# Normalised rows, the mixer's update of X and the copies of last states moved from GpSimd to ScalarE

## The reference

```python
x = x + attn(_layernorm(x), Wq, Wk, Wv, Wo)     # 16 heads; keys: a window of 32 rows, and every 64th row
x = x + ffn(_layernorm(x), k0, k1, k2, s0, s1, s2)
x = x + mamba(_layernorm(x), ...)               # returns its own input plus the output: x appears twice
x = x + ffn(_layernorm(x), k0, k1, k2, s0, s1, s2)

def ffn(x): h = concat([x, -x]); 256 -> 512 -> 512 -> 128, weights of +1 and -1, relu(h) * 2 between
def mamba(x):                                    # E = 256 channels, N = 16 states
    xn = layernorm(x) * ln_g + ln_b
    u, z = split(xn @ W_in);  u2 = silu(causal_conv4(u) + conv_b)
    dt_lo, B, C = split(u2 @ W_xp);  dt = softplus(dt_lo @ W_dt + b_dt)
    h_t = exp(dt_t * A) * h_(t-1) + (dt_t * u2_t) * B_t        # for each of 256 x 16 states, t = 0..1023
    y_t = sum over states of h_t * C_t
    return x + res_scale * (((y + u2 * D) * silu(z)) @ W_out)
```

## Time and profile before

| | |
|---|---|
| median of 3 runs | 812.72 us (811.11 to 813.23) |
| the profiled execution | 811.52 us, of which the trace spans 809.7 |
| busy over the span | PE 89%, DVE 86%, POOL 82%, ACT 73% |
| granted TensorE clock, mean | 0.989 |
| DMA | 154.94 MB, 191 GB/s, 71.4% of 16 engines' span on the main queue |
| first scan starts, last scan ends | 129.8 us, 784.0 us |

### The profile page before, as it was taken

The page is one execution under the profiler, slowest core; times in us unless marked ns, Lnnn a source line. Parts: engine busy times, 40 slices in busy tenths (PEclk is TensorE's granted clock), DMA queues, the critical chain, the costliest instruction groups (busy, mean ns, idle before and its releaser), DMA issues. The chain is left out here.

```text
span 809.7 us, 22189 instructions
## 1 busy us (share of the span) xinstructions
PE 721.4 (89%) x7840; PEld 430.6 (53%) x7840; DVE 695.3 (86%) x1187; ACT 594.8 (73%) x1161; POOL 664.2 (82%) x824
## 2 busy tenths in 40 slices
PE   5999988998789999998999999899896889897887
PEld 3765655644455447545555456355452356453566
DVE  6977229999999989999889999999998989799983
ACT  5776698797788989887689978868667744764533
POOL 5143437998899989989999799899998999999961
PEclk9999999999999999999999999999999999998999
DMA  5000019888799668877777889889797899898950
GB/s 200 3 3 2 2 54 269 226 231 229 206 225 237 159 173 238 230 177 200 198 213 197 225 233 243 232 230 244 207 253 199 252 259 240 215 266 235 264 158 27
DMA packets 84177, 154.94 MB, mean 191 GB/s; under 512 B 9433, under 2 KB 10082, under 8 KB 84066
## 3 DMA queue, kind: packets, MB, share of 16 engines
q1 hardware_dynamic: 84066, 153.51, 71.4%
HBM read 142.46 MB, written 11.01 MB: 190 GB/s over the span
## 5 line engine op out<-in xcount | busy, mean ns | idle before, releaser
L1779 POOL TENSOR_TENSOR d<-d,cr 128x1024 f32<-128x1024 f32 x128 | 300.0, 2354 | 13.8 <-DVE d L1279 4.1
L1578 ACT ACTIVATE ps<-dt,An 128x512 f32<-128x512 f32 x256 | 173.7, 690 | 71.9 <-DVE d L1279 60.5
L1279 DVE TENSOR_TENSOR_SCAN d<-ps,hl,d 128x512 f32<-128x512 f32 x128 | 157.0, 1262 | 3.7 <-ACT ps L1578 3.3
L1279 DVE TENSOR_TENSOR_SCAN d<-ps,d 128x512 f32<-128x512 f32 x128 | 149.6, 1202 | 7.2 <-ACT ps L1578 6.5
L1267 DVE TENSOR_TENSOR d<-ps,d 128x512 f32<-128x512 f32 x184 | 118.5, 671 | 7.1 <-DMA d<-dud 7.1
L891 PE MATMUL ps<-h,w 128*128 128x512 f16 (+1 forms) x512 | 114.3, 373 | 3.5 <-DVE h L1224 2.8
L1766 POOL TENSOR_TENSOR d<-d,br 128x512 f32<-128x512 f32 x72 | 91.5, 1277 | 4.3 <-DMA d<-dud 4.3
L891 PEld LDWEIGHTS ps<-h,w 128*128 128x128 f16 x512 | 46.8, 98 | 70.9 <-DVE h L1224 12.8
L966 PE MATMUL ps<-d,cst 128*32 128x512 f32 x512 | 69.3, 614 | 10.6 <-POOL d L1779 6.4
L1434 ACT COPY pt<-ps 128x512 f32<-128x512 f32 x96 | 53.8, 589 | 13.9 <-PE ps L825 10.6
L825 PE MATMUL ps<-cst,sx 128*128 128x128 f32 x384 | 56.3, 281 | 8.0 <-ACT sx L1427 3.5
(11 more groups left out here) (182 smaller groups left out, 1457.1 us busy)
## 6 DMA issues: line engine op xcount, KB each, us to landing
dt<-dtd SPq DMA_DIRECT2D x256, 256.0 KB, 5.3
d<-dud SPq DMA_DIRECT2D x256, 256.0 KB, 4.8
dtd<-sR SPq DMA_DIRECT2D x16, 256.0 KB, 4.4
dud<-sE SPq DMA_DIRECT2D x16, 256.0 KB, 3.8
X<-in_x SPq DMA_DIRECT2D x8, 256.0 KB, 6.3
br<-bcd SPq DMA_DIRECT2D x8, 256.0 KB
cr<-bcd SPq DMA_DIRECT2D x8, 256.0 KB
out<-X SPq DMA_DIRECT2D x3, 512.0 KB, 5.8
```

The source lines that it names most:

```text
L1279: eng.tensor_tensor_scan(d, banks[u % NG][:, :], d, hl[:, r:r + 1] if m % 2 else 0.0, ALU.mult, ALU.add).then_inc(v_sc, 1)
L1578: eng.activation(banks[u % NG][:, :], DT[:, u % NT, :], ACT.Exp, scale=An[:, g:g + 1]).then_inc(s_da, 1)
L1779: eng.tensor_tensor(d, d, CR[m % 2][:, :].unsqueeze(1).to_broadcast((128, n, 512)), ALU.mult).then_inc(p_cm, n)
```

## The change

- From the third FFN pass on, and for all attention halves but the second of sequence 0, ACT alone normalises the rows (four groups instead of two); POOL only works out scale and shift. `SHARED` names the first two FFN passes, which stay split.
- The mixer's rows are normalised by ACT alone too; its update of X leaves `mln_p` and becomes a step of ACT, `mxu_s`, with places of its own.
- The copy of the last states leaves `out_p` and becomes a step of ACT, `hl_s`, for each pair of units where m is even; `out_p` now waits for it.
- Semaphores follow: `p_mno`, `p_mxa` and `p_hl` are gone, `s_mxa` and `s_hl` are new; the waits for buffers that stood ahead of POOL's rows stand ahead of ACT's.
- All of `PLACES` and `WARM` have new numbers (149 warming products instead of 152). The split of the multiplications by B, the buffers, the loads and all other arithmetic stay.

```diff
+SHARED = FFN_ORDER[:2]
...
-    (HALVES, 'bp_s mln_p mln_s mln_t mln_v mno_s mx_d mx_s mx_t mz_s mz_t silu_s'),
+    (HALVES, 'bp_s mln_p mln_s mln_t mln_v mno_s mxu_s mx_d mx_s mx_t mz_s mz_t silu_s'),
...
+    ([(u,) for u, in PAIRS if u // NR % 2 == 0], 'hl_s'),
...
 def ano_s(b, h):
-                for k in range(4 * h, 4 * h + (2 if b or h else 4)):
+                for k in range(4 * h, 4 * h + (2 if (b, h) == (0, 1) else 4)):
...
 def fno_s(f):
-                for k in range(n // 2):
+                for k in range(n // 2 if f in SHARED else n):
...
 def mno_s(m):
                 eng.wait_ge(p_mrs, 7 * m + 5)
-                for k in range(2):
+                if m:
+                    eng.wait_ge(t_md, 2 * m)
+                    eng.wait_ge(l_bc, 16 * m)
+                for k in range(4):
                     t = eng.activation(LNM[:, k, :], X[:, 4 * m + k, :], ACT.Identity, bias=c[:, k:k + 1], scale=a[:, k:k + 1])
                 t.then_inc(s_mno, 1)
...
+            def mxu_s(m):
+                c1, r1p = mr[:, 3, :], mr[:, 5, :]
+                eng.wait_ge(s_mno, m + 1)
+                eng.wait_ge(p_mrs, 7 * m + 7)
+                for k in range(4):
+                    xk = X[:, 4 * m + k, :]
+                    t = eng.activation(xk, xk, ACT.Identity, bias=c1[:, k:k + 1], scale=r1p[:, k:k + 1])
+                t.then_inc(s_mxa, 1)
...
+            def hl_s(u):
+                r = u % NR
+                eng.wait_ge(v_sc, u + 2)
+                eng.copy(hl[:, r:r + 2], D[:, u % ND:u % ND + 2, 511]).then_inc(s_hl, 2)
...
 def fln_p(f):
                 scales("f", 0, p_frs, 4 * i)
-                if f[2] == 1.5:
-                    eng.wait_ge(t_sc, NU * NB)
-                elif i:
+                if f not in SHARED:
+                    return
+                if i:
                     eng.wait_ge(t_ftr, i)
...
 def mln_p(m):
                 if m:
-                    eng.wait_ge(t_md, 2 * m)
-                    eng.wait_ge(l_bc, 16 * m)
-                    eng.wait_ge(p_mxa, m)
-                    eng.wait_ge(s_mno, m)
+                    eng.wait_ge(s_mxa, m)
...
-                eng.wait_ge(p_mrs, z + 5)
-                for k in range(2, 4):
-                    t = eng.tensor_scalar(LNM[:, k, :], X[:, x0 + k, :], a[:, k:k + 1], c[:, k:k + 1], ALU.mult, ALU.add)
-                t.then_inc(p_mno, 1)
-                eng.wait_ge(p_mrs, z + 7)
-                for k in (2, 3, 0, 1):
-                    if k == 0:
-                        eng.wait_ge(s_mno, m + 1)
-                    t = eng.tensor_scalar(X[:, x0 + k, :], X[:, x0 + k, :], r1p[:, k:k + 1], c1[:, k:k + 1], ALU.mult, ALU.add)
-                t.then_inc(p_mxa, 1)
...
 def out_p(u):
                 eng.wait_ge(v_sc, u + n)
                 if m % 2 == 0:
-                    eng.tensor_scalar(hl[:, r:r + 2], d[:, :, 511], 1.0, 0.0, ALU.mult, ALU.add).then_inc(p_hl, 2)
-                    eng.wait_ge(p_hl, NR * (m // 2) + r + 2)
+                    eng.wait_ge(s_hl, NR * (m // 2) + r + 2)
                 eng.tensor_tensor(d, d, CR[m % 2][:, :].unsqueeze(1).to_broadcast((128, n, 512)), ALU.mult).then_inc(p_cm, n)
```

## The result

The changed kernel takes 892.4 us (median of 4 runs, 890.7 to 895.9) where the kernel before takes 813.0 on the same chip (811.1 to 814.4). The ratio is 1.098, 95% interval 1.093 to 1.103. I had said 800, range 788 to 823. The direction was wrong, and the loss, 79 us, is more than eight times that of the slower case I had worked out (822).

A forecast was written before the change was run, and what follows sets the result against it. It took PE, DVE and POOL as nearly full, with DVE waiting for POOL from 600 to 750. Gains of 7 and 7 us, less 0.8 (tail) and 0.5 (start), 13 rounded, took 811.52 to 798.5; plus 1.2, 800 us, range 788 to 823.

The forecast's parts named there:

- the slower case: Rival: ACT becomes the bound from 250 to 450 us, added work lengthening that stretch by 16.5 us; 822 us, chance 0.28.
- The new places: Order of steps on all engines: nearly the old one, first scan up to 5 us later; cost 0.5 us, ends 0 and 5.
- The gain of 14 us: DVE's idle time among the scans: 7 us back from 600 to 750, 7 us from the other stretches.
- The relief of POOL and the work added to ACT: Busy time over the program: POOL falls to near 613 us, ACT rises to near 641.
- The rows' cover: Normalisations on ACT hand over 0.78 us later, about 25 times; DVE's scans and products cover it: 0, at worst 20 us.
- The copy's hand-over: POOL's product waits for ACT's copy of last states: 0.2 us of delay is hidden, several us at a pair isn't.
- The update of X: Mixer's X step on ACT: needed only tens of scans later, so place free; at mixer 5, 0.9 us beyond two banks' cover.
- The case of no change: Rival: DVE's gaps change their releaser and not their length; 812.7 us, within 0.3%, chance 0.15.
- The rule of the Trainium skill: Optimise the engine with highest occupancy first: DVE at 86% against POOL's 82, so the change would leave about 812 us.
- DVE's share from 600 to 750: Sign in the profile after: DVE's busy share from 600 to 750 us rises from 89% to about 94%.

The follow-up runs named there:

- e1: Changed code with the places of the kernel before, the copy ranked at its pair's second scan end, X step right behind the mixer's rows: 840.6 us, 1.034.
- e9: Changed kernel with its new places, POOL's product by C cut to 8 of 512 columns in even halves: 812.0 us, 0.996.
- e5: Kernel before with its places, only the copies of last states moved to ACT: 812.8 us, 1.000.
- e10: e1 (changed code, old places) with the product by C cut to 8 of 512 columns in even halves: 839.7 us, 1.029.
- e6: Kernel before with its places, only the normalised rows moved to ACT: 823.1 us, 1.013.
- e8: Changed kernel with its new places, but the copies of last states back on POOL inside the product: 887.2 us, 1.092.
- e2: Changed kernel with its new places, only the copies on ACT re-ranked to where their pair's second scan ends: 874.7 us, 1.077.
- e7: Kernel before with its places, only the mixer's update of X moved to ACT, right behind the mixer's rows: 827.6 us, 1.018.
- e11: e1 with the mixer's X step on ACT ranked 6000 units behind the mixer's rows, but for the first: 830.5 us, 1.019.

## Why the prediction was wrong

**The step that failed** is "The new places": "They are nearly the same", and "I take 0.5 us, with 0 and 5 as the ends". Measured: some 52 us (after against e1). I had counted how many scans stand ahead of each step. That finds a step that moved far and misses what decides here: how far a consumer stands behind its producer. It moved by one product, 2.2 us, and in a kernel whose engines run in order that is enough to stop PE 24 times. The diff held the evidence: 149336, 149527, 149718 against 2.35 us for the product. The count of scans was rough as well: by it the first product by C already stood eight scans later, and some of PE's steps moved by 6 or 7 scans, not "one group of four at most". The start too was mis-sized: the first scan starts 9.7 us later, not "up to 5", and in the changed kernel these are not given back behind it. POOL's timeline in the changed kernel shows the first product by C behind a product by B that waits 7.56 us for its load; the kernel before had the first product at 135.09:

```profile
149.50 1.28 POOL L1782 TENSOR_TENSOR d<-d,br 128x512 f32<-128x512 f32 x1 [7.56 <-DMA d<-dud]
...
152.54 4.68 POOL L1794 TENSOR_TENSOR d<-d,cr 128x1024 f32<-128x1024 f32 x2
```

e9 has the same late start (139.3 us) and the same wait of 7.56 us for that load, and yet its last scan ends at 783.3, where that of the kernel before ends at 784.0. So the late start alone need not cost anything.

**The gain of 14 us** was wrong as well. It read DVE's waits for POOL (6.7 us) as time that a lighter POOL gives back. e5 gives POOL the copies' time for 0 us, e10 136 us for 1 to 4. Neither in the kernel before nor in e1 did a lighter POOL pay; that DVE's 6.7 us came from the order in which things are asked for is likely, and not shown.

**The relief of POOL and the work added to ACT** were right: 614.3 and 631.5 us against 613 and 641. ACT came out 10 lower than I said.

**The rows' cover.** "I take nothing for it, with 20 us as the price if the cover is gone." It was half gone: 10 us (e6), with 12 waits of PE of 0.94 and, in e6 alone, POOL's new wait for ACT's rows. I had looked for cover on DVE, while the first to wait is PE, whose list has the transposes next.

**The copy's hand-over.** Hidden, as said (e5: 1.000). The 47.6 us of POOL waiting for it made it look guilty; e8 cleared it as the main cause. Under the new places its ranks cost something (e2: 18 us).

**The update of X.** "its place is free" with 0.9 us over: measured 15 us right behind the rows (e7); 10 of them come back when it stands 6000 units of rank later (e11 against e1), which leaves some 5. In the changed kernel its places stand 1730 to 25318 units of rank behind the rows, so of this cost the smaller part is likely in it; that wasn't tried by itself there.

**The rivals.** The slower case went by ACT as the bound from 250 to 450, 822 us. ACT does have 94.6 of 100 us from 250 to 350, but this stretch is the least disturbed of all. The direction was right for another reason, and the time 70 us short. The case of no change holds for POOL's freed time taken by itself (e5, e10). The rule of the Trainium skill named there (Perfetto Trace Analysis, Identifying the Most-Contended Engine) agrees with these two runs and not with e9, where taking work from POOL, 69% busy in the changed kernel against DVE's 79, gave 80 us back. What decided here shows in no share of busy time: the changed kernel has DVE, ACT and POOL less full and is 10% slower. Of what I said the profile would show, DVE's share from 600 to 750 is 85%, not 94.

**What stays open.** How much of the 52 us is the late first scan (at most some 6 us of it, 139.5 against 133.2 in e1), and how far the dt chain, the loads and PE's clock each carry the delay on, was not separated. e9 at 812 beats e10 at 840 by 28 us with equal work, so the new order is better than the old one for the changed code if its even products are short; whether one laid out for 2.36 us would beat 813 is not known.

## What to carry to other kernels

Where the order is a list of numbers, compare for each producer and its consumers the distance of their ranks with the duration in the trace, engine by engine, and not only who stands ahead of whom; a distance far shorter than the producer's record is a stall already written down. A wait in the profile names the last releaser, not the cause: cut the suspected work once where the order has no room for it and once, by the same amount, where it has. And a busy share of 80% doesn't say that taking work away will pay: find first who waits for that work, and then whether the time falls when it is cut.

## What the runs showed of the hardware

TensorE's clock makes the stalls dearer. The reduction of four units, eight matmuls, takes 1.07 us at 572.93 and 1.94 us at 595.51 and 600.12 in the changed kernel. From 570 to 574 the granted clock is 1.00, from 595 to 598 and from 600 to 603 it is 0.50, that is 2.4 GHz and its lower level of 1.2 GHz. The reduction at 758.10 above, 1.94 us too, falls in another stretch at the lower level, 757.6 to 761.0. Three lines of PE's timeline:

```profile
572.93 1.07 PE L979 MATMUL ps<-d,cst 128*32 128x512 f32 x8 [0.35 <-POOL d L1794]
595.51 1.94 PE L979 MATMUL ps<-d,cst 128*32 128x512 f32 x8 [3.46 <-POOL d L1794]
600.12 1.94 PE L979 MATMUL ps<-d,cst 128*32 128x512 f32 x8 [2.67 <-POOL d L1794]
```

By the clock records of the traces, the changed kernel has 18 stretches at the lower level, 106 us in all; the kernel before has 5, 18 us, and e9 has 4, 34 us. In the changed kernel 11 of the 18 begin during one of PE's waits for POOL's product of 1.8 to 5.2 us, or at most 1.5 us behind its end. That fits stalls that bring the clock down, but not one for one: the clock had fallen at 590.3, ahead of the two waits shown above, and it stayed at 1.00 through the first reduction, behind a wait of 2.00 us.

Over the program one matmul of the reduction takes 702 ns instead of 614, and PE's busy time is 29 us more, though it issues six matmuls fewer. In e9, with the waits gone, it is back at 724.3 us and 625 ns. What part of the 79 us is the clock's can't be read from this, since PE isn't always what the others wait for.
